# A cross-attention and mixture-of-experts kernel: full-height passes in the last shared step, a reordered second norm, a split last expert tile

## What is computed

```python
x = x + xattn(layernorm(x), ctx_512, Wq, Wkv_expand, Wout)     # causal softmax per head
x = x + ffn(layernorm(x), gate_weight, gate_up, down, shared_gate_up, shared_down)
# ffn:
scores = softmax(x @ gate_weight.T); topk_w, topk_idx = top_k(scores, 2)
gu = einsum('th,efh->tef', x, gate_up);  act = silu(gu[..., :352]) * gu[..., 352:]
y  = einsum('tef,te,ehf->th', act, combine, down)
sgu = x @ shared_gate_up.T; sact = silu(sgu[:, :704]) * sgu[:, 704:]
y  = y + sact @ shared_down.T
```

## Time and profile before

| | us |
|---|---|
| three runs | 372.49, 372.67, 370.49 |
| median | 372.49 |
| profiled execution: its time | 370.16 |
| profiled execution: span, first to last instruction | 368.3 |
| busy: PE / DVE / ACT / POOL | 340.6 / 255.7 / 234.2 / 91.0 |
| mean granted TensorE clock | 0.989 of full speed |

### The profile page before, as it was taken

One profiled execution on the slowest core, in us unless ns is written; L12 is line 12 of the kernel. 1 busy time (PEld: TensorE's weight loads), 2 busy tenths in 40 slices (PEclk: granted clock), 3 DMA queues, 4 the chain that ended last, 5 costly groups with the idle time before them and its releaser, 6 DMA issues.

```text
span 368.3 us, 6770 instructions
## 1 busy us (share of the span) xinstructions
PE 340.6 (92%) x2192; PEld 275.8 (75%) x2193; DVE 255.7 (69%) x460; ACT 234.2 (64%) x611; POOL 91.0 (25%) x106
## 2 busy tenths in 40 slices
PE   5599899898999999999999999999999999999971
PEld 5477777676677588798896788888887887888750
DVE  2994886888875518782676797778778778777810
ACT  3525988999995422512226287887887888888720
POOL 3648222322231000054600002211311311221131
PEclk9899999999999999999999999999999999999997
DMA  7999000000000669995779743443354344344233
GB/s 228 365 368 368 17 2 2 3 2 0 3 3 2 239 205 394 372 381 202 253 248 209 266 128 82 64 79 85 59 85 86 57 76 90 64 68 79 52 40 46
DMA packets 28457, 49.45 MB, mean 134 GB/s; under 512 B 6672, under 2 KB 11792, under 8 KB 27408
## 3 DMA queue, kind: packets, MB, share of 16 engines
q1 hardware_dynamic: 24288, 39.91, 33.0%
q0 software_dynamic: 4144, 9.23, 14.2%
HBM read 32.22 MB, written 16.92 MB: 133 GB/s over the span
## 4 chain that ended last, share of the span: by engine, by line
PE 69%; ACT 13%; DVE 7%; DMA 5%; issue 3%; POOL 1%; POOLq 0%; SPq 0%; ACTq 0%; DVEq 0%
PE bank L495 29%; PE bank L774 21%; PE bank L789 9%; ACT prob L876 8%; DMA out<-y_sb,dest 3%; PE bank L678 2%; ACT probT L831 2%; PE bank L664 2%; PE bank L796 2%; DMA w_kv<-wkvT 2%; DVE x2T_lo L1088 1%; DMA w_sg<-sguT 1%; PE bank L487 1%; PE bank L710 1%; PE bank L709 1%
## 5 line engine op out<-in xcount | busy, mean ns | idle before, releaser
L1088 DVE TENSOR_TENSOR gu_parts<-w_gu,gu_parts 128x704 fp32r<-128x704 f32 x84 | 72.8, 887 | 22.9 <-ACT gu_parts L831 21.4
L831 ACT ACTIVATE gu_parts<-w_gu 128x704 fp32r x84 | 66.1, 790 | 15.0 <-PE bank L774 14.6
L774 PE MATMUL bank<-gu_parts,xsT_hi 128*128 128x352 f32 x336 | 69.8, 329 | 0.0
L476 POOL DMA_INDIRECT out<-y_sb,dest x21 | 33.0, 1571 | 147.9 <-ACT y_sb L1028 143.9
L774 PEld LDWEIGHTS bank<-gu_parts,xsT_hi 128*128 128x128 f32 x336 | 55.3, 189 | 0.5 <-issue 0.5
L774 PE MATMUL bank<-gu_parts,xsT_lo 128*128 128x352 f32 x168 | 40.8, 324 | 0.0
L789 PE MATMUL bank<-w_dn,actT_plain 128*128 (+1 forms) x84 | 39.6, 592 | 0.0
L495 PE MATMUL bank<-x2T_hi,w_sg_lo 128*128 128x512 f32 (+1 forms) x88 | 32.2, 366 | 0.1
L495 PE MATMUL bank<-x2T_hi,w_sg_hi 128*128 128x512 f32 (+1 forms) x88 | 32.0, 363 | 0.0
L495 PE MATMUL bank<-x2T_lo,w_sg_hi 128*128 128x512 f32 (+1 forms) x88 | 31.9, 362 | 0.0
L774 PEld LDWEIGHTS bank<-gu_parts,xsT_lo 128*128 128x128 f32 x168 | 29.3, 189 | 0.0
(11 more groups left out here) (191 smaller groups left out, 749.9 us busy)
## 6 DMA issues: line engine op xcount, KB each, us to landing
w_gu<-guT SPq DMA_DIRECT2D x8, 1408.0 KB, 9.5
xs_dram<-xs_in SPq DMA_DIRECT2D x1, 5460.0 KB, 20.4
xs_in<-xs_dram SPq DMA_DIRECT2D x21, 256.0 KB, 2.6
w_dn<-dnT SPq DMA_DIRECT2D x8, 512.0 KB, 6.2
w_sg<-sguT SPq DMA_DIRECT2D x10, 256.0 KB, 5.7
xres<-x SPq DMA_DIRECT2D x2, 768.0 KB, 9.5
w_dn<-dnT SPq DMA_DIRECT2D x8, 192.0 KB, 6.5
w_sd<-sdnT SPq DMA_DIRECT2D x5, 256.0 KB, 6.8
```

Source lines behind the costliest of these rows:

```text
L476: pool.indirect_dma_start(out=out[:, :], out_offset=bass.IndirectOffsetOnAxis(ap=dest[:, i, 0:1], axis=0), in_=y_sb[i % 2][:, :], in_offse ...
L774: ins = pe.matmul(dst[:, 0:F], xsT[x_][:, c, :], gu2[w_][:, c, f0:f0 + F], start=c == 0 and n == 0, stop=c == C - 1 and n == 2)
L831: act.activation(dst, src, ACT.Copy).then_inc(s[sem], 1)
L1088: dve.tensor_tensor(lo_, src, hi_.bitcast(F32), ALU.subtract).then_inc(s[sem], 1)
```

## The change

It has four parts. In the last shared step the pass over 64 rows runs over all 128 (`act_p` whole, and the `lo` weight split over all partitions), which adds the product of the two `lo` parts; the waits for the half chunk move behind the first three passes of each tile. In attention ACT splits `x2T_hi` directly after the first group of exponentials, DVE splits `x2T_lo` between the row maxima of groups 2 and 3; the copy of v goes to DVE for all batches and stands, with `oT_lo`, before the normalisation of group 1. The second norm of row tiles 0 to 4 is applied on POOL instead of DVE. For the last expert tile the weight split comes before the activation, the plain passes come before the split ones, the output is made in two halves in two banks and scaled half by half, and 13 transposes with no use for their result are put in front of and behind `t_act`.

```diff
             pool.iota(token, [[P, NX], [0, 1]], base=0, channel_multiplier=1).then_inc(s["tok"], 1)
+            def apply2(n):
+                pool.wait_ge(s["rs2b"], n + 1)
+                pool.tensor_scalar(x2n[:, n, 0:H], xres[:, n, :], mv2[:, n, 0:1], rstd2[:, n, :],
+                                   ALU.subtract, ALU.mult).then_inc(s["x2n"], 1)
+
             for n in range(NB):
 ...
                     rstd(n - 3, "st2", var2, rstd2, mv2, "rs2a", "rs2b")
+                    apply2(n - 3)
                 for r in range(RP, R):
 ...
                 pe.wait_ge(s["sact_lo"], NBLK * j + t + 1)
-                if j == ND - 1:
-                    pe.wait_ge(s["wsd_hi"], NJ)
-                    pe.wait_ge(s["wsd_lo"], NJ)
-                    pe.wait_ge(s["sact_hi"], NBLK * ND + t + 1)
-                    pe.wait_ge(s["sact_lo"], NBLK * ND + t + 1)
                 for i in range(XB[t])[tiles]:
 ...
                         cols = slice(n * P, (n + 1) * P)
-                        w = FSK[ND][1]
-                        pe.matmul(out_bank[i][:, :], act_p[0:w, cols], w_sd2[SD_BUF[ND]][1][0:w, :], start=False, stop=False)
+                        pe.wait_ge(s["wsd_hi"], NJ)
+                        pe.wait_ge(s["wsd_lo"], NJ)
+                        pe.wait_ge(s["sact_hi"], NBLK * ND + t + 1)
+                        pe.wait_ge(s["sact_lo"], NBLK * ND + t + 1)
+                        pe.matmul(out_bank[i][:, :], act_p[:, cols], w_sd2[SD_BUF[ND]][1][:, :], start=False, stop=False)
                         ins = pe.matmul(out_bank[i][:, :], act_p[:, cols], w_sd2[SD_BUF[ND]][0][:, :], start=False, stop=True)
 ...
                 ins.then_inc(s["edn"], 1)
+
+            def last_down(i, e):
+                for half, bank_ in enumerate((A, D)):
+                    cols = slice(half * H // 2, (half + 1) * H // 2)
+                    at = half * H // 2
+                    pe.wait_ge(s["aT"], i + 1)
+                    for k, (_, w) in list(enumerate(FK))[1:]:
+                        pe.matmul(bank_[:, 0:H // 2], actT_plain[0:w, k - 1, :], w_dn[0:w, bass.ds(e * DN + (k * H + at), H // 2)],
+                                  start=k == 1, stop=False)
+                    for what in ("aT_hi", "aT_lo", "dn_hi", "dn_lo"):
+                        pe.wait_ge(s[what], i + 1)
+                    product(bank_[:, 0:H // 2], [(both(actT_split, every, every), both(dn2, every, cols))], start=False)\
+                        .then_inc(s["edn"], 1)
+
+            def fill_with_transposes(bank_, times):
+                for _ in range(times):
+                    pe.transpose(bank_[:, 0:P], ident[:, :], ident[:, :])
 ...
             gate_up(NT - 1, range(1, C))
+            pe.wait_ge(s["sres"], NX * ND)
+            fill_with_transposes(CC, 8)
             t_act(NT - 1)
+            fill_with_transposes(CC, 5)
             pe.wait_ge(s["ey"], NT - 1)
-            down(NT - 1, e_last[1])
+            last_down(NT - 1, e_last[1])
 ...
                     exps(b + 1, 0)
+                if b >= 3:
+                    put_x2T(b - 3, CC)
                 for r in range(2 if b == 0 else 1, R):
                     put_pT(b, r)
-                    if r == 2 and b >= 3:
-                        put_x2T(b - 3, CC)
                 if b + 1 < NB:
 ...
                 if b + 1 < NB:
-                    if b >= 2:
-                        put_v(b + 1)
                     exps(b + 1, 2)
 ...
+            def put_last_y(i):
+                for half, bank_ in enumerate((A, D)):
+                    act.wait_ge(s["edn"], i + 1 + half)
+                    if half == 0:
+                        act.wait_ge(s["yst"], 16 * (i - 1))
+                    ins = act.activation(y_sb[i % 2][:, half * H // 2:(half + 1) * H // 2], bank_[:, 0:H // 2], ACT.Copy,
+                                         scale=dest[:, i, 1:2].bitcast(F32))
+                ins.then_inc(s["ey"], 1)
+
+            def put_last_actT(i):
+                act.wait_ge(s["Ta"], i + 1)
+                w = FK[-1][1]
+                act.activation(actT_plain[:, 0, :], B[:, P:2 * P], ACT.Copy)
+                act.activation(actT_plain[0:w, 1, :], B[0:w, 2 * P:3 * P], ACT.Copy).then_inc(s["aT"], 1)
+                hi(actT_split[0][:, :], S[3][:, 0:P], "aT_hi")
+
             def put_actT(i):
 ...
                     put_y(i - 1)
+                    dn_hi(e, i)
+                    silu(i)
+                    put_last_actT(i)
+                    break
                 silu(i)
-                if i + 1 < NT:
-                    xs_hi(i + 1)
-                    gu_hi(e_next, i + 1, C - 1)
+                xs_hi(i + 1)
+                gu_hi(e_next, i + 1, C - 1)
                 if i == 0:
 ...
                 e = e_next
-            put_y(NT - 1)
+            put_last_y(NT - 1)
 ...
             def sd_lo(j):
-                at = (slice(0, FSK[j][1]), slice(None))
+                at = (whole, whole)
                 lo(w_sd2[SD_BUF[j]], w_sd[SD_BUF[j]][at], "wsd_hi", j + 1, "wsd_lo", at)
 ...
                     masked(b + 1, 2)
+                if b >= 3:
+                    x2T_lo(b - 3, CC)
+                if b + 1 < NB:
                     masked(b + 1, 3)
 ...
                     put_kT(b + 1)
-                if b >= 3:
-                    x2T_lo(b - 3, CC)
                 if b == 2:
 ...
                         put_kT(3)
+                    put_v(b + 1)
+                oT_lo(b)
+                if b == NB - 1:
+                    apply2(NX - 2)
+                if b + 1 < NB:
                     normalised(b + 1, 1)
-                if b >= 2:
-                    apply2(b - 2)
-                oT_lo(b)
-                if b + 1 < NB:
-                    if b < 2:
-                        put_v(b + 1)
                     normalised(b + 1, 2)
 ...
                         gu_lo(e_next, i + 1, c)
+                if i == NT - 1:
+                    dn_lo(e, i)
                 expert_act(i)
 ...
                         gu_lo(e_next, i + 1, c)
-                dn_lo(e, i)
+                    dn_lo(e, i)
                 aT_lo(i)
```

## The result

| | before | after |
|---|---|---|
| median of four runs each, us | 371.91 (370.49 to 372.67) | 365.26 (364.78 to 366.52) |
| profiled execution, us | 370.16 | 365.72 |
| its span, us | 368.3 | 364.0 |

The account below looks back on a forecast made before the run. ScalarE (ACT) was taken to set the attention period, 9.53 us. Attention 2.5, last shared step 1.8 and last expert tile 0.5 sum to 4.8 us, from the mean 371.45 to 366.7; range for eight in ten 364.0 to 369.8.

Parts of the forecast that it names:

- Attention, 2.3 us for four periods: Attention, batches 2 to 6: the period falls from 9.53 to 8.95 us, 0.58 us for each of four periods.
- the loop that was walked: Attention period: DVE 4.93 us, ACT 2.34, PE 1.28 and 0.4 for three hand-overs, 8.95 in all, DVE the largest part.
- Rival 2: Attention: DVE is not the loop, ACT's floor of 8.5 us holds and 4.3 is gained, 364.9 in all; chance 0.12.
- Batch 6 to 7, 0.15: Attention period set by PE: only 0.15 us of PE's 0.47 us wait for `x2T_lo` goes.
- POOL's application, 0.7, bounds to 1.18: Second norm on POOL: assumed 0.7 us; at 1.18 the period is 9.28 and four periods gain 1.0 us.
- nearer the first, because only one tensor is read: POOL's application of the norm: 0.7 us, nearer a one-input cast (0.47 for 512 columns) than a two-input subtraction (1.18).
- Each 0.1 us above goes straight into DVE's loop: Attention: a POOL application under 0.85 us costs nothing; beyond that DVE's second normalisation waits and lengthens the loop equally.
- rivals 1 and 4: POOL's application holds DVE in attention: at 1.2 to 1.4 us, 368.3 (chance 0.20); at 2.5 us, slower, 373.5 (0.05).
- Last shared step, 1.7 + 0.1: Last shared down step: first expert tile 1.7 us sooner, limited by DVE's `xsT_lo`, 1.4 idle on PE; seventh tile 0.1.
- Tail, 0.5: Last expert tile: reordered passes and two halves end the last scaling about 0.6 us earlier; 0.5 taken, bounds 0 and 0.57.
- The floor: Tail: the last transfer cannot be issued before the previous landing plus 0.71 us, 361.34, or 0.57 us below the profiled issue.
- Nothing takes the 2.5 back: After attention: everything, loads and scatters too, follows from its last output projection, so attention's 2.5 us gain stays whole.

## Why the prediction was right, and where not

The forecast was 366.7 us, the result 365.26, inside the range, and faster as the likeliest case said. The parts came out right in kind, but several steps inside them did not, and errors cancelled. Point by point:

1. *Attention, 2.3 us for four periods: right in kind, too small.* Measured 3.14 from the first product to the seventh, and all of it lies in these four periods. The step "DVE, not ACT, becomes the chain's largest part" failed by a little: the loop that was walked, 8.95, is 8.77 by the estimate above, because I took 4.93 us from the residual sum to the end of the first maximum where the rows give 97.98 + 0.56 - 93.71 = 4.83, and closed it through PE's output projection, while it closes through `x2T_lo` (100.58, 0.23 us behind ACT). So it is within 0.04 of ACT's 8.73, and ACT waits for no maximum. Rival 2's mechanism, with a period of 8.76 instead of 8.5, is what happened. The way of walking the loop was sound: with the application back on DVE it gives 9.22 and ACT waits for the maximum.
2. *Batch 6 to 7, 0.15:* measured 0.45. The whole 0.47 wait went, not a part of it.
3. *POOL's application, 0.7, bounds to 1.18: wrong by three times.* The step "nearer the first, because only one tensor is read" took a cast as the model. In these rows the form decides, not the number of tensors: two scalars per partition cost 2.08 where two tensors cost 1.04. The Trainium skill's figure (GPSIMD Engine Reference, "Performance versus the Vector engine"), an estimate of 0.44 us, was further off still; the traces decide against it for this form.
4. *"Each 0.1 us above goes straight into DVE's loop" (above 0.85), and with it rivals 1 and 4: wrong.* By that step 2.09 us would have made the kernel slower. DVE's normalisation at 97.35, 0.72 us after POOL's start, ran in 0.62. The stall of the earlier trace rows and the one of 2.29 us in the routing are behind a POOL *subtraction of two tensors*; behind a `tensor_scalar` only some 0.45 us near its start were seen. The normalisation begins just behind that time (0.72 us after POOL's start, against the estimated 0.50 to 0.67), which nothing in the forecast had provided for. The rule of the Trainium skill (SBUF — State Buffer, "Who interferes with whom": the second one waits for the whole instruction) fits the first kind in this case and not the second. Two errors, in size and in mechanism, cancelled: that POOL's application cost nothing was luck.
5. *Last shared step, 1.7 + 0.1: right.* Measured 1.85 and 0.09, with idle PE of 1.18 us (forecast 1.4) and `xsT_lo` behind it. Moving that one split ahead took the idle time away, so it was DVE's queue.
6. *Tail, 0.5:* measured 0.31 and 0.28. The floor, 351.90 + 4.70 for the landing + 0.71 = 357.31, is missed by 0.40: ACT waits 0.75 us for the second half's passes. The last transfer was still released by ACT, which the forecast had named as a sign of being wrong. "The last scaling ends about 0.6 us earlier" was too much: counted from the issue of the last transfer but two it ended 0.32 earlier (361.64 - 350.41 = 11.23 before, 357.43 - 346.52 = 10.91 after).
7. *"Nothing takes the 2.5 back":* true in the run with attention alone, false by 1.26 us in the profile of after, where one load was late. In the eleven profiles late loads come and go with the order of the loads unchanged, so a single late load is no verdict on the change. Whether the change makes them more frequent is not shown: six of the eight profiles of kernels with the new attention order and the old order of loads have one, and the kernel before has a single profile, without.
8. *The sum, 4.8 from a base of 371.45.* By the stretches, leaving the 1.26 out, the change gains 3.14 + 0.45 + 1.94 + 0.3 = 5.8 us; with the late load the two profiles differ by 4.44. The medians differ by 6.65 in the result and by 371.53 - 365.84 = 5.7 beside each other on one chip, so the parts account for the change only to about 1 us. From the profiled 370.16 the sum gave 365.4, which is 0.14 from the result; from the mean of the runs, which was taken, 366.7, which is 1.4 from it. That the lower base came so close is luck: the sum was 1 us short, and the late load took about as much back.

## What to carry over

Before a lone operation is moved to another engine, find a row of the same form there, and where the trace has none, as here, time the form first: twice the operands can be half the price. When a load stands in front of a short critical chain in an engine's queue, compare several profiles before a lost microsecond is put down to a change. And where a faster engine ends in a wait, look at the order in the queue that it waits for: moving `xsT_lo` in DVE's order gave 1.3 us here, and nothing else became late.

## Not expected

In these runs GpSimd takes 2.08 us for a `tensor_scalar` with two scalars per partition over 128x512, 1.93 with two constants, 1.63 with one constant operation and 1.04 for a product of two tensors. And the same engine held VectorE in two ways: until the end of a two-tensor subtraction (0.22 became 2.29 us), but for only some 0.45 us near the start of a `tensor_scalar` that runs for 2.08.
